# ViT layer on one core: the attention phase with split scores and turned features, top-two by max and max_index, expert weights split one phase earlier, and images 4 to 14 written out

## The reference

```python
h = tok_ref(x, ...)                        # three patch embeddings, interpolated, mixed: (16, 256, 192)
# attention on n = layernorm(h), 12 heads of 16, random features
q, k, v = split(n @ w_inp + b_inp)
s = einsum('bhld,fd->bhlf', t * d**-0.25, omega)         # t = q or k, 16 features
feat = F**-0.5 * (exp(s - sum(s)/2 - max(s)) + EPS)      # max over a head's features (q), over all heads' (k)
rhs = cumsum(kf * v);  a = (rhs @ qf) / (cumsum(kf) @ qf + EPS)
h = h + a @ w_out + b_out
# experts on x = layernorm(h)
probs = softmax(x @ gate_w + gate_b);  topv, topi = top_k(probs, 2);  topv /= sum(topv)
h = h + sum over 2 experts of topv * (gelu(x @ w1[e] + b1[e]) @ w2[e] + b2[e]) + bk_scale * spectral(x @ v_w)
```

## Time and profile before

| what | us |
|---|---|
| median of 3 runs | 936.08 |
| the profiled execution, its own time | 934.5 |
| span of that execution | 932.8 |
| tokens block, and loads of the attention block | 0 to 95 |
| attention block, working | 95 to 542 |
| experts block | 549 to 933 |

### The profile page before, as it was taken

How to read it: one execution, slowest core, us unless ns; L and a number is a source line. 1 busy time by engine, 2 the same in 40 slices (tenths; PEclk the granted TensorE clock), 3 DMA queues, 4 the chain that set the end, 5 groups by cost and what they waited for, 6 DMA issues and landing times. The chain is left out here.

```text
span 932.8 us, 17076 instructions
## 1 busy us (share of the span) xinstructions
PE 764.9 (82%) x4751; PEld 657.9 (71%) x4752; DVE 547.5 (59%) x1729; ACT 403.9 (43%) x821; POOL 447.1 (48%) x441
## 2 busy tenths in 40 slices
PE   3970689999999999999999306999997899999950
PEld 2560467786767777776767306999997899999950
DVE  2130344676766777676666624888789665565530
ACT  1130343433444444343433004777765566656630
POOL 7733222244444333334442333777775666666542
PEclk9795589888888888898888558999999999999995
DMA  7122211111111121111100002333332234434337
GB/s 169 21 76 98 84 39 58 59 57 33 46 47 49 58 58 58 58 58 58 49 21 21 20 9 58 55 62 63 56 63 40 46 66 77 75 77 76 61 44 138
DMA packets 62448, 55.07 MB, mean 59 GB/s; under 512 B 24616, under 2 KB 55791, under 8 KB 62399
## 3 DMA queue, kind: packets, MB, share of 16 engines
q0 software_dynamic: 19840, 23.53, 14.8%
q1 hardware_dynamic: 38079, 27.77, 10.6%
q10 hardware_dynamic: 4480, 3.21, 1.0%
HBM read 32.52 MB, written 25.10 MB: 62 GB/s over the span
## 5 line engine op out<-in xcount | busy, mean ns | idle before, releaser
L1079 POOL DMA_INDIRECT result<-e_y,e_tag x78 | 137.6, 1764 | 97.1 <-DVE e_y L1408 85.2
L478 POOL DMA_INDIRECT tbl_dram<-a_entry,a_slot x64 | 63.4, 991 | 200.5 <-DVE a_token L926 163.0
L1137 PE MATMUL e_yp<-x_w2s,e_hh 128*128 x468 | 139.4, 365 | 2.0 <-DVE e_y L1408 2.0
L1401 DVE TENSOR_TENSOR e_hl<-e_hid,e_hh 128x512 fp32r<-128x512 f32 x117 | 80.2, 689 | 88.7 <-ACT e_hh L1203 88.5
L1195 ACT ACTIVATE e_hid<-e_hidden,e_b 128x256 f32<-128x256 f32 x234 | 101.2, 475 | 55.0 <-PE e_hidden L1124 39.9
L1138 PE MATMUL e_yp<-x_w2s,e_hl 128*128 x468 | 117.5, 251 | 0.0
L517 PE MATMUL a_s<-a_qb_t,a_kf_t 128*128 128x512 f32 x192 | 110.4, 705 | 0.0
L529 PEld LDWEIGHTS a_ab<-a_values,a_masked 128*128 128x128 f32 x768 | 95.4, 192 | 6.8 <-issue 4.5
L1203 ACT CAST e_hh<-e_hid 128x512 fp32r<-128x512 f32 x117 | 72.4, 621 | 61.8 <-PE e_yp L1138 61.8
L1067 POOL DMA_INDIRECT e_x<-x_dram,e_tag x78 | 81.7, 1048 | 36.3 <-issue 22.9
L529 PE MATMUL a_ab<-a_values,a_masked 128*128 (+1 forms) x768 | 95.0, 256 | 0.6 <-DVE a_masked L768 0.6
(11 more groups left out here) (254 smaller groups left out, 1619.6 us busy)
## 6 DMA issues: line engine op xcount, KB each, us to landing
a_raw_c<-in_ew SPq DMA_DIRECT2D x16, 288.0 KB, 3.1
h_dram<-t_hs SPq DMA_DIRECT2D x4, 768.0 KB, 4.2
a_hb<-h_dram SPq DMA_DIRECT2D x16, 192.0 KB, 2.7
a_raw_a<-in_ew SPq DMA_DIRECT2D x16, 192.0 KB, 2.4
a_raw_b<-in_ew SPq DMA_DIRECT2D x32, 96.0 KB, 2.6
result<-a_hb SPq DMA_DIRECT2D x16, 192.0 KB, 2.0
x_dram<-a_att SPq DMA_DIRECT2D x16, 192.0 KB, 2.0
spec_dram<-e_space ACTq DMA_DIRECT2D x16, 192.0 KB, 2.0
```

Of the source, the lines that this page charges most:

```text
L1079: pool.indirect_dma_start(out=out, in_=y[:, j], in_offset=None, out_offset=bass.IndirectOffsetOnAxis(ap=tag[:, i % 8, j, 0:1].bitcast(U32) ...
L1137: pe.matmul(Y[:, j, 0:2 * D], hh[:, f, c], w(f, 2 * D), start=f == 0, stop=False, skip_group_check=True)
L1401: g.tensor_tensor(hl[:, f:f + 2].rearrange("p f t -> p (f t)"), hid[:, f:f + 2].rearrange("p f t -> p (f t)"), hh[:, f:f + 2].rearrange("p ...
```

## The change

The functions are edited as follows.

1. **Loop**: rounds 4 to 14 are written out by `for i in range(4, B)` instead of `Fori`; no register addresses remain in the attention block.
2. **Scores**: the exponentials are kept unpadded (16 a head). ACT adds EPS, and writes each as a rounded high part in `split`, POOL writes the low part f - high. A head has three slots: high, low, high for queries, and high, high, low for keys (in f32r, the format that PE reads in one pass). Two heads give 96 rows, which are turned by a matmul against the identity in f32r (`turn_keys`, `turn_queries`, 6 per half and kind, 24 an image instead of 12). `score` is then two f32r matmuls of 256 columns instead of one f32 matmul of 512, six times an image. ACT copies the queries twice, times a 0/1 column (`own_head`), 768 columns each, where it wrote 32-partition blocks. The state takes six heads at once (2 matmuls instead of 3).
3. **Choice**: `top_two` and `choose` take the two largest logits with MAX and MAX_INDEX; the second's weight is exp(gap). `place` has 9 instructions. The prefix is 4 small matmuls on bf16.
4. **Weights**: the split of w1 moves into the tokens block, where ACT makes high parts and DVE low parts, expert by expert, ahead of the copies of groups t1, p2 and p1; the raw rows lie in `hs`. w2 stays in the attention block.
5. **Order**: the steps of a round are interleaved anew on PE, ACT, DVE and POOL; the copy of the values moves from DVE to ACT; DVE makes the state at the end of a round.

```diff
-            with eng.Fori(4, B - 1) as i:
+            for i in range(4, B):
                 emit(i, True, True, True, True)
-            emit(B - 1, True, True, True, True)
...
+        weights_before = {("t1", 0): (0,), ("t1", 1): (0,), ("p2", 0): range(1, NE), ("p1", 0): range(1, NE)}
...
+                for e in weights_before.get((what, k), ()):
+                    weights(e)
...
+                    if k < 2:
+                        eng.wait_ge(w1_low, 2 * NE)
...
+            def low_part(i, j):
+                wait_apart(pool, s["hi_ready"], 4 * i + 2 * j + 2)
+                for n, c in ((0, 1), (1, 2)):
+                    own = slice(n * H, (n + 1) * H)
+                    g.tensor_tensor(split[j][:, own, c], feat[j][:, own], split[j][:, own, 0].bitcast(F32), ALU.subtract
+                                    ).then_inc(s["lo_ready"], 1)
...
-                        pe.matmul(S[j][:].rearrange("p h t -> p (h t)"), kf_t[:, g, j * P:(j + 1) * P],
-                                  qb_t[:, g, j].rearrange("p h t -> p (h t)"), start=True, stop=True
-                                  ).then_inc(s["s_done"], 1)
...
+                    if n < 2:
+                        pe.wait_ge(s["kT_out"], TJ * b + j + 1)
+                        pe.wait_ge(s["qT_out"], TJ * b + j + 1)
...
+                    for p in range(2):
+                        last = pe.matmul(S[j][:, 2 * p:2 * p + 2].rearrange("p h t -> p (h t)"),
+                                         kf_t[:, 2 * g + p, j * P:(j + 1) * P],
+                                         qb_t[:, 2 * g + p, j].rearrange("p h t -> p (h t)"), start=True, stop=True)
+                    last.then_inc(s["s_done"], 1)
...
+                def turn_keys(j):
+                    for n in range(NP):
+                        last = pe.matmul(FB[0:CF, n * P:(n + 1) * P],
+                                         split[j][:, H + 2 * n:H + 2 * n + 2].rearrange("p h c f -> p (h c f)"),
+                                         ident_r[:], start=True, stop=True)
+                    last.then_inc(s["kT_done"], 1)
...
+                    act.activation(feat[j][:], feat[j][:], ACT.Exp).then_inc(s["exp_done"], 1)
+                    act.wait_ge(s["exp_done"], 4 * i + 2 * j + 1)
+                    act.activation(feat[j][:], feat[j][:], ACT.Identity, bias=eps_col[:, 0:1]).then_inc(s["exp_done"], 1)
...
+                    for n, at in ((0, slice(0, 3, 2)), (1, slice(0, 2))):
+                        own = slice(n * H, (n + 1) * H)
+                        act.copy(split[j][:, own, at], feat[j][:, own].unsqueeze(2).broadcast_to([P, H, 2, NF])
+                                 ).then_inc(s["hi_ready"], 1)
...
+                    for r in range(2):
+                        last = act.activation(qb_t[:, :, j, r], FA[0:CF, 0:NP * P].rearrange("p (n t) -> p n t", n=NP),
+                                              ACT.Copy, scale=own_head[:, r:r + 1])
+                    last.then_inc(s["qT_out"], 1)
...
+                for j in range(TJ):
+                    v.max(out=best[:, j], in_=lg[:, j, 0:NE]).then_inc(s["found"], 1)
+                wait_apart(dve, s["found"], 4 * b + 2)
+                for j in range(TJ):
+                    v.max_index(out=where[:, j], in_max=best[:, j], in_values=lg[:, j, 0:NE]).then_inc(s["found"], 1)
```

708 lines of the change are left out of this document (356 added, 352 removed).

## The result

| | before | changed |
|---|---|---|
| median of 4 runs, us | 936.1 (935.7 to 937.3) | 959.9 (947.5 to 965.1) |
| ratio, 95% interval | | 1.021 (1.011 to 1.031) |
| profiled execution, us; its span | 934.5; 932.8 | 960.8; 959.0 |
| attention block begins (first DMA of its SyncE) | 74.9 | 80.6 |
| state of the first image, of the last | 116.5, 497.1 | 122.3, 523.5 |

The changed kernel is slower, by 1.1 to 3.1%; the forecast was 873.6, with a range up to 909. The 26.2 us between the two spans are 5.7 in the tokens block, 20.6 in the 15 intervals (401.2 against 380.6), -2.4 from the last state to the experts block, 2.2 in the experts block, and 0.1 in the first image.

A forecast was written before the change was run, and what follows sets the result against it. PE was taken to bound the attention block: 18.0 work + 1.3 wait + 0.5 gaps + 1.7 clock = 21.5 us an image against 25.4. With -58.5 + 3 - 8 + 1 = -62.5 us, forecast 873.6 us, range 844 to 909.

The forecast's parts named there:

- PE's work: Attention block, one image: PE's work at full clock falls from 20.7 to 18.0 us.
- ACT: Attention block: ACT needs 13.0 us an image, well under PE's 18, but its query copies come late in the round.
- The wait of 1.3 us at the end of a round: Attention block: PE waits 1.3 us once a round for ACT's query copies of half 1; small gaps add 0.5.
- Clock: Attention block, after the wait at a round's end: 3.4 us at half speed, costing 1.7 us an image.
- Rival (c): Averages, gate and turns, without a dense score between, keep the clock low: 1076 us, slower from 25.7 an image; chance 0.07.
- rival (a): Attention block: the clock stays up, image 19.8 us, 848 us in all; chance 0.2.
- The rule on transposes: Transpose-mode matmuls don't count as busy for the clock, so 24 turns as plain matmuls would now count; no size given.
- The loop written out: Eleven more rounds of attention written out cost 0 us, at most some 10 if instruction blocks came late.
- Tokens block: Weight splitting moved here: +1 us, bounds 0 and +15; ACT and DVE mostly wait, the 6.3 MB load can be late.
- Ends: First image +3 us; after the last state -8 us, from shorter scores, choice chain and gate.
- Experts block: Experts block stays as long as before, 384 us.
- Rival (b): Attention block: waits and clock cost more, image 22.9 us, 895 us in all, up to 909; chance 0.25.

The follow-up runs named there:

- e16: Changed kernel with its 24 turns an image as f32 transposes instead of f32r matmuls: 900.7 us, 0.941 of the kernel before, 21.6 us an image.
- e4: Separate kernel without the computation, PE running one matmul kind after another, some 40 us each, from a high clock; averages fell to 0.50 after 5.6 us, total not given.
- e13: Separate kernel without the computation, testing which matmul kinds restore a low clock: transposes after 5.5 us, f32r turns not in 24.1 us; total not given.

## Why the prediction was wrong, point by point

- **PE's work.** 18.0 us an image; the changed kernel's round holds 17.0, and e16's round at full clock takes 19.1 (295.26 to 314.35 us), less 0.8 of waits and 0.5 for transposes 17.8. Right. Inside the sum a pair of scores took 0.33 us from start to start (319.07 to 319.40) and not 0.24; a turn 0.086 (32.6 us for 380 in e4), not the 0.108 taken.
- **ACT.** The query copy of 96 x 768 took 0.89 us where 0.88 was taken, POOL's low part 0.59 for 0.55. The wait of 1.3 us at the end of a round did not come, nor the 0.5 for small gaps: PE waits 0.2 us there in the changed kernel and 0.4 twice in e16, released by DVE's state first, not by ACT's copies:

```profile
L745 ACT ACTIVATE a_qb_t<-a_fa,a_own_head 96x768 fp32r<-96x768 f32 x64 | 53.9, 893 | 31.8 <-PE a_fa L590 31.8
L486 POOL TENSOR_TENSOR a_split<-a_feat,a_split 128x192 fp32r<-128x192 f32 x64 | 36.7, 594 | 104.8 <-ACT a_split L730 104.8
```

- **Clock: the step that failed.** It took one low spell of 3.4 us a round, 1.7 us of cost, because the falls in the earlier trace rows followed a waiting PE and a full PE had brought the clock back. Measured: 20.5 us low, 10.2 us of cost. "A full PE brought it back each time" took PE's busy time for what counts. In the row 141.9 to 145.3 PE was full of dense matmuls; full of averages and f32r turns it stays at 1.2 GHz (e4, e13). That is 8.5 us more than forecast for the clock; 1.6 of waits that did not come, 1.0 of work and 0.6 for the two shorter intervals at the start stand against it, which leaves about the 5.2 us an image that are missing (26.7 against 21.5). They are 79 of the 89 us between forecast and profiled time. Rival (c) named the place (averages, gate and turns without a dense score) and set its threshold at 25.7 us; it had 0.07. It took the whole round to be low (35 us), it was three quarters. It counted the turns among the short matmuls that lose the clock, rightly, where rival (a) counted them for a clock that stays up; what neither had is that transposes in their place would bring the clock back.
- **The rule on transposes.** Rival (a) leaned on the Trainium skill (TensorE: Matmul & The Clock Gate, Part 4: PE-mode transpose), by which the full clock doesn't engage for matmuls in transpose mode, since they don't count as busy the same way (its times there are for bf16; these are f32). The runs differ: 380 transposes held 1.00 for 41.4 us, and begun at 0.50 they brought the clock back 5.5 us after their start; it is the plain f32r turns that did not. The measurement decides, and with it goes the support that rival (a) took from this rule.
- **The loop written out.** Taken at 0. A round is as long either way; the loop version was 0.993 of before against 1.021 and 1.024, in part by rounds that escape the low clock. Not settled.
- **Tokens block.** +5.7 for +1, inside the bounds 0 to 15. What can be late was said to be the load; DVE's and ACT's order puts the weights ahead of the copy of p2, and this was the part called mostly idle.
- **Ends.** First image +0.1 us (41.7 before and after, from the block's begin) for +3. Tail -2.4 for -8. The choice chain did better than taken, 2.8 us (557.36 to 560.17) against 7.3 before (529.02, one row ahead of the earlier trace rows, to 536.30): -4.5 for -3.4, with MAX8 and FIND_INDEX8 at 0.16 to 0.18 us each. But the clock is 0.50 from the last state on, and PE's busy time in the tail is 27.2 us where it was 24.2:

```profile
523.50:560.20 36.70, 27.18 (x124) 25.07 (x123) 14.21 (x71) 4.01 (x8) 9.76 (x12) 0.50 0.09 25
```

- **Experts block.** 2.2 us longer, taken as equal. Its clock is 0.91 in the mean against 0.93 before; it begins low and stays so until 594.2 us.
- **The upper end of the range.** Rival (b) at its longest adds up to 18.0 + 1.8 + 0.5 + 3.4 = 23.7 us and 907 us, not 23.9 and 909. It changes nothing in the outcome.

e16 takes 21.6 us an image, and the forecast said 21.5. That is luck: e16 is another kernel, its low clock costs it 3.0 us an image (5.9 us low in the mean) where 1.7 was forecast, and its waits are 0.6 where 1.8 was. What holds of the sum is PE's work.
